# A graph network kernel: the first sixteen first-stage tiles gather rows of x itself, and 48 such tiles stand where 40 stood

## What is computed

```python
def rgcn_conv(x, edge_index, edge_type, W, root, bias):
    out = x @ root + bias
    for r in range(8):
        mask = edge_type == r
        msg = jnp.where(mask[:, None], (x @ W[r])[src], 0)
        agg = jax.ops.segment_sum(msg, dst, num_segments=N)
        cnt = jax.ops.segment_sum(mask.astype(x.dtype), dst, num_segments=N)
        out = out + agg / jnp.maximum(cnt, 1.0)[:, None]
    return out
...
h = jnp.maximum(_layernorm(x, axis=-1), 0.0)
x = x + relu(rgcn3(relu(rgcn2(relu(rgcn1(h))))))
h = jnp.maximum(_layernorm(x, axis=-1), 0.0)
aggr = jax.ops.segment_sum(h[src], dst, num_segments=n)
z = jax.nn.relu((h + aggr) @ W1 + b1) @ W2 + b2
x = x + batchnorm(z) * gamma + beta + h
```

## Time and profile before

| | us |
|---|---|
| median of three runs | 1883.6 |
| lowest and highest | 1880.57, 1884.61 |
| the profiled execution | 1885.77 |
| its span (first to last instruction) | 1883.8 |
| POOL busy in the span | 1612.1 |
| PE busy | 1277.2 |
| DVE, ACT busy | 888.7, 645.7 |

### The profile page before, as it was taken

The page is one execution under the profiler, slowest core; times in us unless marked ns, Lnnn a source line. Parts: engine busy times, 40 slices in busy tenths (PEclk is TensorE's granted clock), DMA queues, the critical chain, the costliest instruction groups (busy, mean ns, idle before and its releaser), DMA issues.

```text
span 1883.8 us, 18726 instructions
## 1 busy us (share of the span) xinstructions
PE 1277.2 (68%) x4614; PEld 863.5 (46%) x4614; DVE 888.7 (47%) x3270; ACT 645.7 (34%) x1146; POOL 1612.1 (86%) x2502
## 2 busy tenths in 40 slices
PE   7888665657476776666667666675566666667787
PEld 3564444434344554444444344454444444444554
DVE  5784754545442366757676666652222222122213
ACT  5404000000000376867677766732011011112123
POOL 5888888888888888888888888878888888888881
PEclk9987655555555655657565656575567675757678
DMA  7823332323232311213121312231111111111111
GB/s 240 288 81 90 102 116 71 112 72 103 80 90 62 97 46 45 90 46 90 45 90 45 91 45 79 58 96 45 46 45 45 46 45 45 46 45 46 46 46 45
DMA packets 70010, 144.25 MB, mean 77 GB/s; under 512 B 23487, under 2 KB 37048, under 8 KB 69896
## 3 DMA queue, kind: packets, MB, share of 16 engines
q0 software_dynamic: 39840, 81.67, 17.3%
q1 hardware_dynamic: 29624, 60.67, 8.9%
q10 hardware_dynamic: 432, 0.64, 0.1%
HBM read 100.23 MB, written 42.67 MB: 76 GB/s over the span
## 4 chain that ended last, share of the span: by engine, by line
POOL 75%; issue 11%; PE 9%; DMA 4%; DVE 1%; ACT 1%; another core or an unknown queue 0%; POOLq 0%; DVEq 0%; SPq 0%; ACTq 0%
POOL rows L1249 53%; POOL slow L1234 19%; DMA rows<-h_table,idx 3%; PE ps_agg L562 2%; POOL early L1239 2%; PE ps_agg L617 1%; PE ps_a L580 1%; PE ps_h L531 1%; POOL rows L1270 1%; PE ps_agg L591 1%; PE ps_a L669 0%; PE ps_a L649 0%; PE ps_a L603 0%; PE ps_h L669 0%; ACT early L733 0%
## 5 line engine op out<-in xcount | busy, mean ns | idle before, releaser
L1249 POOL DMA_INDIRECT rows<-h_table,idx x1183 | 1127.4, 953 | 199.7 <-issue 190.2
L562 PE MATMUL ps_agg<-sel,rows 128*128 128x64 f32 (+16 forms) x2780 | 734.6, 381 | 452.2 <-DMA rows<-h_table,idx 445.3
L562 PEld LDWEIGHTS ps_agg<-sel,rows 128*128 128x128 f32 x2780 | 638.7, 290 | 725.3 <-DMA rows<-h_table,idx 539.3
L964 DVE TENSOR_SCALAR sel<-iota,early,norm 128x64 f32<-128x64 f32 x1186 | 436.8, 430 | 474.4 <-PE ps_agg L562 451.9
L1234 POOL MEMSET slow<- 128x264 f32 (+1 forms) x1248 | 424.1, 340 | 0.7
L1060 DVE TENSOR_TENSOR early<-ps_a,early 128x300 f32 x416 | 197.5, 475 | 207.9 <-PE ps_a L649 160.9
L846 ACT ACTIVATE scratch<-scratch,ones 128x300 bf16<-128x300 f32 x416 | 222.6, 535 | 119.6 <-PE ps_a L649 96.6
L649 PE MATMUL ps_a<-scratch 128*128 128x300 bf16 x416 | 168.3, 405 | 113.5 <-issue 67.7
L852 ACT ACTIVATE scratch<-iota,code_lo 128x300 f32<-128x300 f32 x416 | 226.5, 545 | 12.5
L531 PE MATMUL ps_h<-w_all,xT 128*128 128x512 f32 x300 | 214.1, 831 | 6.6 <-issue 4.9
L942 DVE TENSOR_SCALAR_CACHE_REDUCE agg_s<-scratch,key_f 128x256 bf16<-128x256 int16 x416 | 194.8, 476 | 7.0 <-DMA scratch<-key_rows 5.5
(11 more groups left out here) (158 smaller groups left out, 760.5 us busy)
## 6 DMA issues: line engine op xcount, KB each, us to landing
h_table<-stage SPq DMA_DIRECT2D x65, 512.0 KB
rows<-h_table,idx POOLq DMA_INDIRECT x1183
scratch<-key_rows SPq DMA_DIRECT2D x26, 544.0 KB
h_table<-scratch SPq DMA_DIRECT2D x10, 512.0 KB
x_rows<-in_x SPq DMA_DIRECT2D x6, 256.0 KB, 6.3
w_all<-in_W SPq DMA_DIRECT2D x3, 512.0 KB, 6.6
x_table<-early SPq DMA_DIRECT2D x6, 256.0 KB, 2.3
out<-early SPq DMA_DIRECT2D x6, 256.0 KB
```

Source lines behind the costliest of these rows:

```text
L562: mm = nc.tensor.matmul(sums_of(L, k)[:, at:at + width], mine, sel[edges, G % SELS, in_window:in_window + width], start=False, stop=(t == ...
L964: done = nc.vector.tensor_scalar(mine, here, dst, weight, ALU.is_equal, ALU.mult)
L1249: pool.indirect_dma_start(rows[:, slot, :], None, table, bass.IndirectOffsetOnAxis(ap=column, axis=0)).then_inc(landed, 16)
```

## The change

`FORE` goes from 40 to 48. The gathers of the first 16 of these tiles read the input x, not x0_table, and POOL waits for x0_table only ahead of the 17th. Those sixteen tiles are normalised where they land: DVE takes statistics of each gathered row (`raw_stats`), ACT the square root (`raw_deviation`, behind its copies of block 6 of table 0), DVE the reciprocal and shift (`raw_norm`), and ACT normalises one tile behind the copies of each of the blocks 8 to 23 (`raw_tile`). PE waits for that in its first sixteen first-stage tiles.

```diff
...
 FILLS = 4
 REGS = 16
 
-FORE = 40
+FORE = 48
+RAW = 16
+RAW_SD_AT = 6
+RAW_AT = 8
 FORE_RING = 12
 FORE_PACE = 2
 FORE_SPAN = 48
...
         count = sb("count", [P, 2, BATCH])
         col_i = sb("col_i", [P, 1], I32)
         rest = sb("rest", [P, 4 * P])
+        raw_stat = sb("raw_stat", [P, RAW, 6])
+        raw_mv = sb("raw_mv", [P, RAW, 2])
+        raw_sd = sb("raw_sd", [P, RAW])
+        raw_rs = sb("raw_rs", [P, RAW])
+        raw_nm = sb("raw_nm", [P, RAW])
         slow = sb("slow", [P, 2, HEAD_PAUSE])
 
 
...
                         pe.wait_ge(s_key_bank, j - A_BANKS + 1)
                     nc.tensor.matmul(ps_a[j % A_BANKS][:], zeros[:, 0:P], zeros[:], start=True, stop=False)
             pe.wait_ge(s_fore_sel, t + 1)
-            pe.wait_ge(s_fore_row[t // BATCH], 16 * BATCH)
+            if t < RAW:
+                pe.wait_ge(s_raw, t + 1)
+            else:
+                pe.wait_ge(s_fore_row[t // BATCH], 16 * BATCH)
             for j, at, in_window, width in key_pieces(t):
                 mm = nc.tensor.matmul(ps_a[j % A_BANKS][:, at:at + width], fore_rows[:, t, :],
                                       fore_sel[:, t % FORE_RING, in_window:in_window + width], start=False,
...
                 done = nc.scalar.activation(xn0[:, b, :], x_rows[:, b, :], ACT.Relu, bias=ln_nm[:, b:b + 1],
                                             scale=ln_rs[:, b:b + 1])
             done.then_inc(s_xn, 1)
+
+        def raw_deviation(act):
+            act.wait_ge(s_raw_mv, 1)
+            nc.scalar.activation(raw_sd[:], raw_mv[:, :, 1], ACT.Sqrt, bias=vecs[:, 7:8]).then_inc(s_raw_sd, 1)
+
+        def raw_tile(act, t):
+            act.wait_ge(s_raw_nm, 1)
+            nc.scalar.activation(fore_rows[:, t, :], fore_rows[:, t, :], ACT.Relu, bias=raw_nm[:, t:t + 1],
+                                 scale=raw_rs[:, t:t + 1]).then_inc(s_raw, 1)
 
         def key_whole(act, j):
 
...
             dve.wait_ge(s_rs, g + 1)
             nc.vector.scalar_tensor_tensor(ln_nm[:, b0:b1], ln_mv[:, b0:b1, 0], -1.0, ln_rs[:, b0:b1],
                                            ALU.mult, ALU.mult).then_inc(s_nm0, 1)
+
+        def raw_stats(dve):
+            for t in range(RAW):
+                if t % BATCH == 0:
+                    dve.wait_ge(s_fore_row[t // BATCH], 16 * BATCH)
+                done = nc.vector.bn_stats(raw_stat[:, t, :], fore_rows[:, t, :])
+            done.then_inc(s_raw_stat, 1)
+            dve.wait_ge(s_raw_stat, 1)
+            for t in range(RAW):
+                done = nc.vector.bn_aggr(raw_mv[:, t, :], raw_stat[:, t, :])
+            done.then_inc(s_raw_mv, 1)
+
+        def raw_norm(dve):
+            dve.wait_ge(s_raw_sd, 1)
+            nc.vector.reciprocal(raw_rs[:], raw_sd[:]).then_inc(s_raw_rs, 1)
+            dve.wait_ge(s_raw_rs, 1)
+            nc.vector.scalar_tensor_tensor(raw_nm[:], raw_mv[:, :, 0], -1.0, raw_rs[:], ALU.mult, ALU.mult
+                                           ).then_inc(s_raw_nm, 1)
 
         def fore_select(dve, t):
 
...
                            channel_multiplier=0).then_inc(s_pool_const, 1)
             nc.gpsimd.iota(iota_i, pattern=[[1, EARLY + NP]], base=-EARLY, channel_multiplier=0).then_inc(s_pool_const, 1)
             pool.wait_ge(s_src, 32)
-            pool.wait_ge(s_x0, 16 * GROUPS)
 
             def rest_a_while(G, words):
 
...
                     done.then_inc(s_rested, 1)
 
             for t in range(FORE):
-                pool.indirect_dma_start(fore_rows[:, t, :], None, x0_table,
+                if t == RAW:
+                    pool.wait_ge(s_x0, 16 * GROUPS)
+                pool.indirect_dma_start(fore_rows[:, t, :], None, x if t < RAW else x0_table,
                                         bass.IndirectOffsetOnAxis(ap=src_i[:, t:t + 1], axis=0)
                                         ).then_inc(s_fore_row[t // BATCH], 16)
                 rest_a_while(t, HEAD_PAUSE)
...
                 for b in range(*x_groups[g]):
                     evacuate(act, nc.scalar.copy, 0, b, 0)
                     evacuate(act, nc.scalar.copy, 0, b, 1)
+                    if b == RAW_SD_AT:
+                        raw_deviation(act)
+                    if RAW_AT <= b < RAW_AT + RAW:
+                        raw_tile(act, b - RAW_AT)
                 if g == 2:
                     act.wait_ge(s_pool_const, 5)
                     nc.scalar.copy(iota[:], iota_i).then_inc(s_iota, 1)
...
                                            ).then_inc(s_idx, 1)
             dve.wait_ge(s_pool_const, 4)
             nc.vector.tensor_tensor(key_near, key_f[:, 0:FORE], fore_at, ALU.subtract).then_inc(s_near, 1)
+            raw_stats(dve)
+            raw_norm(dve)
             dve.wait_ge(s_total, 1)
             nc.vector.tensor_scalar(flag[:, 0:1], ps_total[:, 0:1], 0.0, None, ALU.is_equal).then_inc(s_flag, 1)
             dve.wait_ge(s_flag, 1)
```

More of the change, by code:

```diff
@@ L416, in gnn_kernel @@
         s_nm0 = sem("s_nm0")
+        s_raw_stat = sem("s_raw_stat")
+        s_raw_mv = sem("s_raw_mv")
+        s_raw_sd = sem("s_raw_sd")
+        s_raw_rs = sem("s_raw_rs")
+        s_raw_nm = sem("s_raw_nm")
+        s_raw = sem("s_raw")
         s_x0 = sem("s_x0")
```

## The result

| | before | changed |
|---|---|---|
| median of five runs each, same chip | 1883.2 | 1873.8 |
| lowest to highest | 1880.6 to 1884.6 | 1872.4 to 1874.7 |
| the profiled execution | 1885.8 | 1873.8 |
| its span | 1883.8 | 1871.9 |

The changed kernel is faster: ratio 0.995, 95% interval 0.9936 to 0.9965, so 6.6 to 12.1 us, 9.4 in the middle. The forecast was 1871.6, between 1868.5 and 1877.0. The time lies in the range; how it came about is not what the sum said, as the profile shows. In a second comparison, on another chip, the same kernel came to 1878.4 against 1884.5: ratio 0.9965, interval 0.9952 to 0.9978, a gain of 4.1 to 9.0 us.

What follows compares the result with a forecast made beforehand. Bound by POOL's gather chain, unless PE holds it back in the head. Gather 78 at 127.5 instead of 140.05 gains 12.5, taken as 12: profiled run 1873.8, less 2.2 for the median, 1871.6 us; range 1868.5 to 1877.0.

Steps and rivals of the forecast that it cites:

- Part 1: POOL's start: first gather at 7.5 against 22.71, 15.2 us earlier; first gather from h_table reached at 80.4.
- Part 2: h_table 0 at POOL's first gather from it: last store lands at 80.3, so no wait; 3.0 lost if 83.4.
- The cap of the gain: POOL's own chain without PE: gather 78 at 124.9 instead of 140.05, so at most 15.1 us gained.
- Part 3: Normalising sixteen raw tiles on DVE and ACT: mostly hidden in idle time, delaying the end of h_table 0 by 0.4 us.
- mechanism D: ACT's in-order queue: square root waits for late raw rows, holding copies and h_table 0; ACT held a few us, mostly this: 0.06.
- the 38.8: Latest end of DVE's raw statistics and aggregates, ahead of ACT's square root; delay was to cost only from 40.7.
- Part 4: PE's rounds in the head: start at 83.6 instead of 86.14, last 42.5 us instead of 35.3, end at 126.1.
- rival B: Head: late rows or table and a slow clock; gain 8.1 us, 1875.5, with all three; chance 0.20.
- Part 5: Hand-over at gather 78: goes out at 127.5 after POOL waits 2.6 us for PE; gain 12.5, taken as 12.
- Part 6: DVE's sixteen extra selectors ahead of tile 56: batch ready about 96.3, PE there about 100, hidden by 4 us.
- Rival C: PE's clock stays at 1.2 GHz through the whole head, rounds end around 140, no gain, 1883; chance 0.07.
- Rival D beyond its point: Raw rows landing later than near 53 hold ACT, making the kernel slower; 1891 at 20 us; chance 0.05.

## Why the prediction was right, and where it was not

By the signs that the prediction itself had named, its working failed although its number held: PE's rounds start after 86 and the clock falls there, two of the three signs of being wrong. The third, POOL's pace behind tile 78, stayed in its bounds (1.467 us a gather up to gather 100).

**Part 1, POOL's start: right.** 7.11 against 7.5 expected. POOL would have been at h_table at 80.2 (82.04 less 1.88); 80.4 was expected.

**Part 2, the table: mis-sized by 1.6 us.** I took the last store to land 7.0 us behind 73.3. The store was given out at about 73.6 and landed at about 81.9, 8.3 us later, and POOL waited 1.88 us. In the nine profiles of changed kernels where POOL waited for it, it went on between 80.95 and 84.02. The cap of the gain was not 15.1 but 13.5 us.

**Part 3, the normalising: the sum came out, a term did not.** The sixteenth raw tile was given out at 30.58 and landed at 37.4, 6.8 us; I had the bounds 2.7 and 5.1. ACT stood 4.04 us before its square root, up to the very moment where its next copy went before. Table 0 was 0.3 us later by PE's last ten half blocks (64.17 against 63.84), and 0.4 was the forecast. That agreement is luck. The cover named there, a copy that could not go before 40.68, was read from the kernel before, whose PE was 1.4 us later at that point; with the wait out of the way a store released that copy at 38.95. So this is mechanism D, already at work when the 38.8 became 40.2, while the prediction had it cost nothing up to 40.7. Three terms give the 0.3: about 1.4 us ahead at block 4, which was not forecast, differs between executions of nearly the same code (block 4 begins between 29.8 and 31.7 us in the runs with raw gathers, at 29.84 here) and stays unexplained; the same 1.4 lost again in the wait; and 0.3 to 0.4 for the four activations ahead of the cast, the one term that came as forecast.

**Part 4, the head on PE: the step that failed.** 83.6 plus 42.5 was to be 126.1; it was 86.6 plus 45.7, 132.3. The 6.2 us by term (the selectors, the other reason given for 83.6, were late too: DVE's key chunk came at 75.32 in place of 73.77 and it began the selector of tile 12 only at 84.11; behind the late rows this cost nothing):

- start, 3.0: 1.6 from the table, 1.4 from the rows, which took 4.6 us from the gather to PE where 3.2 were allowed (2.7 for the landing, the rest for selectors)
- clock, 1.9: I took it off for a pause that would be short. The pause was 3.81 us, and the clock fell. Keeping PE busy gave back 1.94
- the first two rounds at full clock: 3.85 us in place of the 3.2 of later rounds, 0.6. Some 0.2 of it is the opening of a bank, which the later rounds compared do not have, and 0.4 the late rows of the second tile; so some 0.2 of the 1.9 above was never the clock's in the kernel before
- the four more rounds with the opening and the bank sum: 13.9 us from 118.41 to 132.27, where before it was 4.1 from 117.30 to 121.41; 9.8 more, and 9.1 expected, 0.7.

What the Trainium skill says in TensorE: Matmul & The Clock Gate, Part 1, that an idle TensorE drops to half rate, agrees with the rows: 0.50 behind an idle time of 3.81 us, 1.00 with the idle time filled or cut to 0.57. The error lay in the length of the pause and not in the rule. How short a pause is safe the runs do not settle: the clock held behind 0.57, 1.32 and once 2.44 us, and fell behind 1.74 (the raw gathers alone) and 2.62 (20 in the head with late weights).

The row landings were read from the wrong neighbours. The text named the cause as a point for rival B (weights and a chunk on the same DMA engines) and set against it a 7.0 that was the latency of a load of SyncE's own queue; the gathers were given 2.7, read at 83.42 to 86.14 in the kernel before, when that traffic had just run out (DMA share 0.25 in 84 to 86; 0.71 in the changed kernel). The Trainium skill, DMA: Bandwidth & Descriptors, section on queues, has the engines serve the queues in turn, and I took from it that the landing would be near the short end. The run with late weights shows what the traffic does: 2.7 us without it, 4.6 with it. Whether the engines took turns here no run shows; if they did, the gather was still 1.9 us later.

**Part 5, the hand-over: the form right, the size not.** The longest wait is where it was put, at gather 78, and ends 1.26 us behind PE's last bank sum (1.4 expected). Two shorter ones stand at gathers 74 and 76 (1.04 and 1.85 us), where none was expected, from the same lateness. POOL waited 7.0 us in place of 2.6. The gain at gather 78 was 6.5 us, not 12.5. This is rival B, with table, rows and clock, and 1.6 beyond its 8.1.

**What brought the time back into the range.** The medians gave 9.4 us, the head's lead is 6.3. In the second comparison the medians gave 6.1. The two profiled executions differ by 12.0 us (their spans by 11.9), the very 12 that the forecast took off, and that is luck: 6.3 come from the head, 2.9 from behind gather 100, and 2.7 from behind the last gather, where the kernel before took 40.1 us in this profile and 37.3 in its second. The profile of before ran into a wait for table 2 and that of the changed kernel did not; such waits differ from execution to execution in either kernel. So part of the agreement between 1871.6 and 1873.8 is probably chance. The intervals of the two comparisons have 6.6 to 9.0 us in common; that the range held is due to the first one, since 1878.4 lies above its 1877.0 (on a chip where the kernel before took 1884.5).

**Part 6 was right:** no wait for a selector stands in front of tile 56. **Rival C** is out: the clock was at 0.96 in 91 to 95 again. **Rival D beyond its point** did not happen; short of that point D did, for about 1.3 us.

## What to carry to other kernels

When an engine that gives out transfers is started earlier, work out what it reaches early, and whether that is ready: a door (table 0 here) turns an earlier start into a wait, unless there is other work to put in front of it, and that work lands on another engine. Here neither half of the change showed a gain alone. A latency read in a quiet stretch does not hold for the first transfer behind a load; look at what the queues have been given just ahead. A wait of the old kernel is no cover for new work if the change may move the start of that wait. And a lookahead limit is best set stage by stage: 20 tiles in the head saved 7 us, and 20 tiles behind it lost some 8.

## What was not expected

- A gather of 128 rows landed in 2.7, 4.6 or 6.8 us, depending on the traffic of other queues at that time (DMA share 0.16 and 0.79 for the first two).
- A longer lookahead behind the head cost time, in both kernels: 617.4 and 618.9 us from gather 828 to the last, against 607.0 to 612.3. PE ended the layer 19 us behind POOL instead of 7 to 13. Why PE itself came later there (1251.4 against 1244.9 and 1244.0 for the kernel before; 1237.4 against 1231.4 to 1232.4 for the changed kernel with 20 tiles in the head alone) is open; no run went after it.
- The door of table 0 opens at a time that scatters by 3 us between nearly equal programs, one execution each (80.95 to 84.02), more than most of the terms that the sum tried to tell apart.
- The clock fell behind a pause of 1.74 us in one run and held behind 2.44 us in another.
